# Scores of a retention layer in eight array tiles of 32 rows by 64 columns

## What is computed

```python
    attn = jnp.einsum('bihd,bjhd->bhij', q, k) * decay[None] / scale
    y = jnp.einsum('bhij,bjhd->bihd', attn, v)
    mean = y.mean(axis=(1, 3), keepdims=True)
    var = y.var(axis=(1, 3), keepdims=True)
    yn = (y - mean) / jnp.sqrt(var + EPS)
    yn = yn.reshape(b, t, dm) * gn_weight + gn_bias
    return yn @ W_o.T
```

## Time and profile before

| | |
|---|---|
| Median of 3 runs | 445.52 us (444.48 to 446.04) |
| The profiled execution | 445.83 us, of which the span of the profile is 444.0 us |
| Busy in the span | PE 436.3 us (98%), PEld 391.8 (88%), DVE 296.7 (67%), ACT 216.9 (49%), POOL 95.6 (22%) |
| Granted TensorE clock | 1.000 over the span, that is 2.4 GHz throughout |
| Instruction queue (q8) | 44 packets, 0.72 MB |
| Scores (L437), PE | 1,024 passes |

### The profile page before, as it was taken

One profiled execution on the slowest core, in us unless ns is written; L12 is line 12 of the kernel. 1 busy time (PEld: TensorE's weight loads), 2 busy tenths in 40 slices (PEclk: granted clock), 3 DMA queues, 4 the chain that ended last, 5 costly groups with the idle time before them and its releaser, 6 DMA issues.

```text
span 444.0 us, 14549 instructions
## 1 busy us (share of the span) xinstructions
PE 436.3 (98%) x6318; PEld 391.8 (88%) x6318; DVE 296.7 (67%) x685; ACT 216.9 (49%) x416; POOL 95.6 (22%) x73
## 2 busy tenths in 40 slices
PE   6999999999999999999999999999999999999997
PEld 5999998999999999998989988899988999888995
DVE  6887788766877778876656663857548575575433
ACT  3565556545773567535246342472424723346430
POOL 1103223522245023550531100311004020040000
PEclk9999999999999999999999999999999999999999
DMA  7543332222341121325240014100123001120011
GB/s 260 157 133 98 99 98 75 75 68 80 122 121 52 51 97 51 99 98 185 101 142 1 0 50 173 65 0 0 47 98 138 0 0 47 47 94 0 1 47 47
DMA packets 15382, 34.64 MB, mean 78 GB/s; under 512 B 2368, under 2 KB 2656, under 8 KB 14816
## 3 DMA queue, kind: packets, MB, share of 16 engines
q1 hardware_dynamic: 14896, 33.05, 22.5%
q10 hardware_dynamic: 432, 0.79, 0.6%
HBM read 25.44 MB, written 8.40 MB: 76 GB/s over the span
## 4 chain that ended last, share of the span: by engine, by line
PE 96%; DMA 2%; DVE 1%; ACT 0%; issue 0%; ACTq 0%; POOL 0%; DVEq 0%
PE bank L358 52%; PE bank L367 13%; PE bank L437 7%; PE bank L368 7%; PE bank L475 4%; PE bank L466 4%; PE bank L451 3%; PE bank L416 2%; DMA wqkv_raw<-wattn 2%; PE bank L554 2%; PE bank L377 1%; PE bank L491 1%; ACT keo L687 0%; PE bank L481 0%; PE bank L485 0%
## 5 line engine op out<-in xcount | busy, mean ns | idle before, releaser
L770 ACT ACTIVATE xres<-bank,r1b 128x256 f32<-128x256 f32 x64 | 26.8, 470 | 54.9 <-PE bank L368 53.6
L358 PE MATMUL bank<-x2hi,sw_hi 128*128 128x512 f32 x128 | 51.3, 400 | 0.0
L358 PE MATMUL bank<-x2lo,sw_hi 128*128 128x512 f32 x128 | 50.4, 394 | 0.0
L755 ACT ACTIVATE sil<-bank,s1b 128x512 f32<-128x512 f32 x32 | 22.0, 688 | 58.1 <-PE bank L358 58.1
L358 PE MATMUL bank<-x2hi,sw_lo 128*128 128x512 f32 x128 | 50.3, 393 | 0.0
L367 PE MATMUL bank<-sw_both,ghi 128*128 128x512 f32 x128 | 46.5, 396 | 0.0
L367 PE MATMUL bank<-w_both,ehi 128*128 128x512 f32 x128 | 46.4, 397 | 0.0
L865 DVE TENSOR_TENSOR pm<-bank,msk 128x512 f32<-128x512 f32 x64 | 39.8, 683 | 9.2 <-PE bank L437 9.2
L1037 DVE SCALAR_TENSOR_TENSOR gf<-bank,s3b,sil 128x512 f32<-128x512 f32 x32 | 23.9, 748 | 32.1 <-PE bank L358 32.1
L687 ACT ACTIVATE keo<-kT,msk 128x512 f32<-128x512 f32 x32 | 21.4, 714 | 39.6 <-DVE kT L854 39.6
L358 PE MATMUL bank<-xhi,wqkv_hi 128*128 128x256 f32 x128 | 39.3, 307 | 0.6 <-DVE xlo L849 0.5
(11 more groups left out here) (119 smaller groups left out, 1133.1 us busy)
## 6 DMA issues: line engine op xcount, KB each, us to landing
xin<-xa SPq DMA_DIRECT2D x16, 256.0 KB, 3.1
w_raw<-w SPq DMA_DIRECT2D x16, 256.0 KB, 3.1
xres<-xs SPq DMA_DIRECT2D x16, 256.0 KB, 3.3
x_scratch<-xres SPq DMA_DIRECT2D x16, 256.0 KB, 3.1
xl<-x_scratch SPq DMA_DIRECT2D x8, 512.0 KB, 5.2
xr<-x_scratch SPq DMA_DIRECT2D x4, 1024.0 KB, 4.9
out<-xr SPq DMA_DIRECT2D x7, 512.0 KB, 2.6
sw_raw<-sw SPq DMA_DIRECT2D x6, 256.0 KB, 3.6
```

The lines of the kernel that those rows point to most:

```text
L358: mm = nc.tensor.matmul(o, w[c][l], x[c][r], start=first and c == 0 and j == 0, stop=last and c == n - 1 and j == 2)
L755: nc.scalar.activation(sil[i % 2][:], h1_bank[i % 2][:], ACT.Silu, bias=s1b[:, m:m + 1]).then_inc(sil_ready, 1)
L770: ge = nc.scalar.activation(hf[q % 2][:, m, :], e_bank[q % 4][:, m * 2 * P:(m + 1) * 2 * P], ACT.Gelu, bias=r1b[:, e, m:m + 1])
```

## The change

For each chunk and group, the 128 weight columns of a pair are issued as two matmuls of 64, one per head: first the even head of all four pairs, onto partitions 0 to 63 of the banks, then the odd head of all four, onto 64 to 127. The tiles of the array are then 32 rows by 64 columns, eight of them. What is loaded as weights in sum, the results and where they lie are the same, and so are the semaphores; the last matmul still signals `sc_done`. Nothing changes on the other engines.

```diff
                 for c in range(CPS):
                     for g in range(GROUPS):
                         o = (c * GROUPS + g) * CH
-                        for p in range(PAIRS):
-                            at = slice(32 * p, 32 * p + 32)
-                            mm = nc.tensor.matmul(p_bank[p][:, o:o + CH], keo[at, c, g, :, :],
-                                                  qT[h % 2][at, g, c * CH:(c + 1) * CH], start=True, stop=True)
+                        for odd in range(2):
+                            for p in range(PAIRS):
+                                at = slice(32 * p, 32 * p + 32)
+                                mm = nc.tensor.matmul(p_bank[p][CH * odd:CH * odd + CH, o:o + CH], keo[at, c, g, odd, :],
+                                                      qT[h % 2][at, g, c * CH:(c + 1) * CH], start=True, stop=True)
                 mm.then_inc(sc_done, 1)
```

## The result

| | before | changed |
|---|---|---|
| Median of all runs | 445.22 us (444.04 to 446.19) | 457.60 us (456.72 to 461.08) |
| Ratio | | 1.029 (95% interval 1.0261 to 1.0320) |
| Span of the profiled execution | 444.0 us | 454.9 us |
| PE busy in the span | 436.3 us | 434.9 us |

The prediction, 442.7 us with 438.5 to 447.7, is wrong: the kernel got 12.4 us slower. In the lines of the changed kernel all numbers behind the scores are one higher (L452 `state_sums`, L467 `from_state`, L476 `from_scores`). TensorE is busy for less time than before, and "issue", which stood at 0% of the chain, has 3%. The instruction queue shows 52 packets where there were 44.

What follows compares the result with a forecast made beforehand. The prediction took TensorE to bound the kernel: -6.8 us from shorter scores, capped by low_x, and +4.0 us for fetching instructions make -2.8 us, 442.7 us from a median of 445.52, with a range of 438.5 to 447.7.

Steps and rivals of the forecast that it cites:

- What bounds the kernel: Whole kernel: TensorE is 96% of the chain of work that ended last.
- why the scores are dear: Scores: loading 128 weight columns takes some 107 ns and sets a round of four passes, 121 ns.
- The scores after: Scores on eight tiles: 1.15 us per part in place of 1.94, between 1.04 and 1.25.
- sign against the tiles: Scores: if they take over 1.5 us, the tiles are the wrong step.
- cap of 1.47: Scores: at 1.47 us or less the saving stops at 0.47 us per part, since project_k waits for low_x.
- `low_x` is late next: Behind the scores, project_k waits about 0.3 us for low_x; gain capped at 6.6 us over parts 1 to 14.
- Parts 0 and 15: First and last attention parts: ScalarE's copy_v limits the gain to 0.11 us and 0.13 us.
- Instructions to fetch: Unrolled attention stage: 128 more instructions per part, packets of 256 taking 3.3 us, give back 4.0 us.
- discount of 0.7: Fetch term: factor on the computed shortfall, as the old trace had about 0.7 of the 1.7 us reckoned.
- window sum: Attention parts: mean shortfall of 256-instruction windows below 3.3 us, 0.47 us per new part against 0.11 per old.
- rival 2: Unrolled attention stage: instruction supply sets the pace at 3.6 us per packet, +2.8 us, 448.3; chance 0.13.
- Rivals 3 and 4: Scores: tiles sharing rows don't overlap, +2.2 us, chance 0.11; fixed price per pass, +31 us, chance 0.02.

Runs made afterwards that it cites:

- e5: The changed kernel's scores on eight tiles, reading the upper 16 bits of q and k as bfloat16, one pass per matmul: 439.9 us, 0.9872 of the kernel before.
- e6: The kernel before, its scores on four tiles, with the upper 16 bits of q and k read as bfloat16: 439.1 us, 0.9858 of the kernel before.
- e7: The changed kernel with each pair's even and odd head issued right behind each other: 458.3 us, 1.0311 of the kernel before.
- e1: The kernel before with four single-column matmuls of 32 weight columns added ahead of each round of scores: 509.9 us, 1.1447 of the kernel before.
- e8: The kernel before, scores unchanged, with 32 single-column matmuls added ahead of from_state in each part: 472.5 us, 1.0575 of the kernel before.

## Why the prediction was wrong, step by step

- *What bounds the kernel, and why the scores are dear:* the first is right. For the second, the load of 64 columns takes 131 ns in the median, between the 187 and the 105 of the earlier trace rows, as the slope wants it. That the load sets a round was argued and not tested: e5 and e6 changed the number of passes too.

```profile
L438 PEld LDWEIGHTS bank<-qT,keo x2048: 127/131/133, 16.0 to 205.3; 32*64 32x64 f32 x187
```

- *The scores after:* 1.52 us where I took 1.15 with 1.25 as a bound. That is 95 ns for a round of eight in place of 65, and 11.9 ns per pass, so the 9.8 ns that half of `state_sums` shows were not held for 128 passes in a row. What sets it was not tried. It is just over the 1.5 us that the prediction named as a sign against the tiles, but its price is small: 0.05 us above the cap of 1.47, 0.7 us in 14 parts.
- *`low_x` is late next:* right, and shown by e5 and e6. In the changed kernel itself the scores end about where `low_x` does, so the forecast wait of 0.3 us isn't there.
- *Parts 0 and 15:* not looked into further.
- *Instructions to fetch:* this is the step that failed, in its size. The mechanism stood in the prediction, its place too (`state_sums` behind the scores, `from_state`, `from_scores`), and eight more packets came. The term was 4.0 us, and by the whole difference it was some 18: the profiled span grew by 10.9 us though the scores' starts fall 0.42 us per part closer together, 6.7 us. The stops themselves, forecast at 2 to 6 us in all, came to 15.0. Three things in it were off. The time per packet: I took 3.3 us, between a run of 3.15 without a stop and stops at 3.55 and 3.77, and where packet after packet is waited for it is mostly 3.83 to 3.89. The constant: a stop came 3.46 us after the packet's edge (98.85 to 102.31, the edge found by counting back) and another 5.46 (164.44 to 169.90), so long waits stand beside short ones and a mean doesn't price them. And the discount of 0.7, which I had fitted to a kernel that is hardly ever short. The sum also took all 16 parts as some 10.6 us long, which seven of them are.

The run of 3.15 us misled me. The packet behind it started ahead of the edge at 183.75, not after it. The instruction queue from 183.5 to 183.75 us in the kernel before, and from 37.5 to 38.6 in the changed one, where a stop had ended at 36.09 (from 36.1 to 37.5 there is none):

```profile
q8 instruction: 1, 0.02, 29.1%
```

```profile
q8 instruction: 1, 0.02, 5.4%
```

So in the first case the packet was under way before the edge. In the second it began at least 1.4 us after the edge. That it was asked for early while the engine worked off slower matmuls is my reading, and no run tests it. Minimum runs without a stop therefore say little of the supply's own pace; stops that follow each other say more. With 3.85 the window sum gives 1.22 us per part in the changed kernel (with scores of 1.52), and 0.46 in the one before, 12 us apart, and a total near +5. But it gives 7 us of stops for the kernel before, which has about 1, and 20 for the changed one, which has 15.0, so the sum over windows with one fixed time per packet is itself too coarse. What stays open is what sets the start of a packet's transfer, 0.7 to 3.1 us after the entry of the packet before it ahead of those 17 stops, and with it a rule that gets both kernels right.

- *Rivals:* rival 2, the supply sets the pace, is what happened, with 13% and priced at +2.8 us; its threshold (3.4 us per packet) was passed. Rivals 3 and 4 fell: they wanted 2.08 and 3.9 us for the scores. The rule of the Trainium skill weighed in the prediction ("TensorE: Matmul & The Clock Gate", section "Wait — 56ns, not 53.3ns?") fell with them: the scores' passes start 11.9 ns apart on average over eight tiles, where it has a floor of about 25.

## What to carry to other kernels

Count instructions, not only their time: where unrolled code on an engine runs many short ones, compare the time that 256 of them take with the time between stops that follow each other, and look for stops named "issue" that lie a constant number of instructions apart before adding more. Splitting a matmul over more tiles paid here only where its instructions could be fetched in the shorter time; fewer passes gave the gain without that risk, but at the price of bfloat16 operands. And find what the shortened group was hiding: here a copy and a subtraction were reckoned to cap the gain at 0.47 us per part, 6.8 in all, and e5 and e6 gained 5.5 and 6.2.

## What the runs showed of the hardware

- A packet of 16 KB, about 256 instructions of TensorE, came 3.83 to 3.89 us after the one before in four of the five cases where the engine waited for two in a row, some 15 ns per instruction, and 4.81 us after it in the fifth. The stops ended 2.2 to 3.0 us after the start of the packet's transfer.
- After the longest stop of the changed kernel (it ended at 169.90) the granted clock was 0.50, that is 1.2 GHz, from 170.65 to 174.06, which can cost at most 1.7 us; e7 had a stop as long, no such stretch and the same span.
- Eight tiles of 32 by 64 ran 128 passes of 32-bit operands in 1.52 us; four tiles of 32 by 128 ran 64 in 1.94.
- Changing the tile shape seems dear: in e1 two rounds of scores and two of added passes of another shape took 0.55 us where the scores alone took 0.24. The added ones stream a single column, and eight such passes without a change of shape take 0.08 (e8).
